# A gated block in eight steps: GpSimd's low parts behind VectorE's mixes, one low part moved to VectorE, another order in the first step

## The reference

```
emb  = layernorm(x) + ctx
q, k, v = emb@wq + bq, emb@wk + bk, emb@wv + bv
ek   = exp(k - max_t k);  ew = exp(w - max w),  w = pos_bias inside a band of 64
y    = sigmoid(q) * (ew @ (ek*v)) / (ew @ ek)
a    = layernorm(y@wo + bo + emb) * gamma + beta
x1   = x + tanh(g_xattn) * (layernorm(relu(a@w1 + b1)@w2 + b2 + a) * gamma + beta)
xn   = layernorm(x1);  xp = xn shifted down by one row
xk   = mu_k*xn + (1-mu_k)*xp;  xr = mu_r*xn + (1-mu_r)*xp
out  = x1 + tanh(g_ffn) * sigmoid(xr@W_r) * (square(relu(xk@W_k)) @ W_v)
```

## Time and profile before

| | |
|---|---|
| median of 3 runs | 509.66 us (509.17 to 512.01) |
| profiled execution, its own time | 508.8 us |
| its span, first to last instruction | 507.1 us |
| busy: TensorE products, weight loads | 450.7 us (89%), 402.5 us (79%) |
| busy: VectorE, GpSimd, ScalarE | 433.1 (85%), 303.7 (60%), 234.3 us (46%) |
| mean granted clock of TensorE | 0.963 of 2.4 GHz |
| DMA | 48.27 MB, 95 GB/s |

### The profile page before, as it was taken

One profiled execution on the slowest core, in us unless ns is written; L12 is line 12 of the kernel. 1 busy time (PEld: TensorE's weight loads), 2 busy tenths in 40 slices (PEclk: granted clock), 3 DMA queues, 4 the chain that ended last, 5 costly groups with the idle time before them and its releaser, 6 DMA issues. The chain is left out here.

```text
span 507.1 us, 8069 instructions
## 1 busy us (share of the span) xinstructions
PE 450.7 (89%) x2884; PEld 402.5 (79%) x2884; DVE 433.1 (85%) x768; ACT 234.3 (46%) x366; POOL 303.7 (60%) x242
## 2 busy tenths in 40 slices
PE   7889997779979897998979998898979996999986
PEld 7778896669869795997869796897959885897975
DVE  4998779699888999699996999789986997279987
ACT  3581653515264343825255343834255242536353
POOL 2573862386765786675775786665773653744431
PEclk9999999699989999899989999899999997999999
DMA  7742210446023820347114650244212330011002
GB/s 259 241 126 83 63 43 2 129 141 197 1 83 98 244 88 0 106 166 197 41 50 128 189 145 0 91 134 161 84 41 53 124 120 7 1 41 43 2 0 84
DMA packets 44216, 48.27 MB, mean 95 GB/s; under 512 B 8592, under 2 KB 40336, under 8 KB 44176
## 3 DMA queue, kind: packets, MB, share of 16 engines
q1 hardware_dynamic: 43088, 46.18, 29.3%
q10 hardware_dynamic: 1088, 1.57, 1.0%
HBM read 31.29 MB, written 16.45 MB: 94 GB/s over the span
## 5 line engine op out<-in xcount | busy, mean ns | idle before, releaser
L1682 PE MATMUL ps<-w_hi,hid_hi 128*128 128x256 f32 x248 | 61.6, 284 | 0.8 <-issue 0.5
L1682 PE MATMUL ps<-a_hi,w_hi 128*128 128x512 f32 x128 | 52.9, 414 | 9.9 <-DVE hid_lo L1070 7.0
L1682 PE MATMUL ps<-w_lo,hid_hi 128*128 128x256 f32 x248 | 61.0, 282 | 0.0
L1496 ACT ACTIVATE hid_hi<-ps,b 128x512 fp32r<-128x512 f32 x60 | 37.9, 686 | 39.7 <-PE ps L1682 39.7
L923 DVE RECIPROCAL y<-y 128x512 f32<-128x512 f32 x16 | 53.6, 3350 | 0.3
L1682 PE MATMUL ps<-a_hi,w_lo 128*128 128x512 f32 x128 | 52.3, 409 | 0.0
L1070 DVE SCALAR_TENSOR_TENSOR hid_lo<-ps,neg_b,hid 128x512 fp32r<-128x512 f32 x60 | 41.2, 736 | 10.8 <-ACT hid L1502 10.8
L1682 PEld LDWEIGHTS ps<-w_hi,hid_hi 128*128 128x128 f32 x248 | 47.1, 190 | 1.7 <-issue 1.2
L1682 PEld LDWEIGHTS ps<-w_lo,hid_hi 128*128 128x128 f32 x248 | 47.0, 189 | 0.4
L237 POOL TENSOR_TENSOR ek_lo<-y,ek_hi 128x1024 fp32r<-128x1024 f32 x13 | 31.2, 2402 | 21.3 <-ACT ek_hi L1472 21.3
L1682 PE MATMUL ps<-a_lo,w_hi 128*128 128x512 f32 x128 | 36.3, 406 | 4.4 <-POOL a_lo L237 4.4
(11 more groups left out here) (265 smaller groups left out, 1405.8 us busy)
## 6 DMA issues: line engine op xcount, KB each, us to landing
x_in<-in_x SPq DMA_DIRECT2D x8, 512.0 KB, 4.3
emb<-in_ctx SPq DMA_DIRECT2D x8, 512.0 KB, 3.8
x_beta<-in_x SPq DMA_DIRECT2D x8, 512.0 KB, 4.7
out<-out_sb SPq DMA_DIRECT2D x7, 512.0 KB, 4.3
key_room<-norm SPq DMA_DIRECT2D x6, 512.0 KB, 2.6
y<-key_room SPq DMA_DIRECT2D x24, 128.0 KB, 2.9
mid_room<-hid SPq DMA_DIRECT2D x6, 512.0 KB, 2.6
hid<-mid_room SPq DMA_DIRECT2D x24, 128.0 KB, 2.9
```

What stands on the lines that cost most here:

```text
L1496: act.activation(tile(hi, b, T), bank(relu_pair(n, q), b), ACT.Relu, bias=b1[:, m:m + 1]).then_inc(hid_hi_done, 1)
L1682: return pe.matmul(o, s, m, start=start, stop=stop, skip_group_check=True)
```

## The change

On GpSimd the three low parts of a step's middle wait for both of VectorE's mixes (`xr_done`) and run in the order xk, xr, y; `ek_low` waits for `x1_done` and comes after `stats("ff")`; `a_square_low` leaves GpSimd for VectorE, between `scale_ff` and `finish_x1`. On TensorE the wait for `ek_done` moves ahead of `hidden(b,3)` and the wait for the hidden low parts ahead of `values`, and in the last step `hidden(b,2)` comes before `ffn_k`. In the first step (`i == FIRST_MID`) VectorE, ScalarE, SyncE and GpSimd take the attention sum, the mid norm and its turn first and the head norm, the keys' turn and sums after them; `hidden(0,3)` gets other banks, and the counts of the stores follow the new order.

```diff
--- before.py
+++ after.py
@@ -290,15 +290,15 @@
 
         def keys_stored(n):
 
-            return 16 * (STORES * (n - FIRST_EK) + 1)
+            return 16 * (STORES * (n - FIRST_EK) + (2 if n == FIRST_EK else 1))
 
         def sums_stored(n):
 
-            return 16 * (STORES * (n - FIRST_EK) + 2)
+            return 16 * (STORES * (n - FIRST_EK) + (3 if n == FIRST_EK else 2))
 
         def mid_stored(n):
 
-            return 16 * (STORES * (n - FIRST_MID) + 3)
+            return 16 * (STORES * (n - FIRST_MID) + (1 if n == FIRST_MID else 3))
 
         def emb_stored(n):
 
@@ -381,7 +381,9 @@
 
             if is_last(n):
                 return (0, 2, 1, 0)[q]
-            return (0, 2, 1, 0)[q] if isinstance(n, int) and n == BATCH - 2 else (0, 2, 0, 0)[q]
+            if n == 0:
+                return (0, 2, 0, 1)[q]
+            return (0, 2, 1, 0)[q] if n == BATCH - 2 else (0, 2, 0, 0)[q]
 
         def value_pair(n):
 
@@ -561,12 +563,16 @@
                 load_unit(sp, u)
 
             def step(i, p):
-                if has(i + 1):
+                if i == FIRST_MID:
+                    load_ctx(i + 2, p)
+                    spread_mid(i)
                     spread_keys(i + 1)
                     spread_sums(i + 1)
-                if has(i + 2):
-                    load_ctx(i + 2, p)
-                if mid_squares(i):
+                elif not is_last(i):
+                    spread_keys(i + 1)
+                    spread_sums(i + 1)
+                    if has(i + 2):
+                        load_ctx(i + 2, p)
                     spread_mid(i)
                     sp.wait_ge(mid_landed, mid_moved(i))
                 if has(i + 2):
@@ -703,13 +709,14 @@
                     emb_plus_bo(d, 1 - p)
                 if has(a):
                     delta_of(pool, a)
-                if has(a) and is_last(i):
+                if has(a):
+                    pool.wait_ge(xr_done, DC * (a + 1))
                     xk_low(pool, a)
                     xr_low(pool, a)
                 y_low(pool, i)
-                if has(a) and not is_last(i):
-                    xk_low(pool, a)
-                    xr_low(pool, a)
+                if i == FIRST_MID:
+                    stats("mid", i)
+                    scale_a(i, p)
                 if has(e):
                     stats("head", e)
                 if has(a) and is_last(i):
@@ -717,18 +724,19 @@
                 x_plus_beta(b)
                 if has(a) and not is_last(i):
                     sq_low(pool, a)
-                stats("mid", i)
+                if i != FIRST_MID:
+                    stats("mid", i)
                 if has(e):
                     pool.wait_ge(norm_done["mid"], TT * (i + 1))
                     make_emb(pool, e, p)
-                scale_a(i, p)
+                if i != FIRST_MID:
+                    scale_a(i, p)
                 if is_last(i):
                     finish_a(i, p)
+                stats("ff", b)
                 if has(d):
+                    pool.wait_ge(x1_done, TT * (b + 1))
                     ek_low(pool, d)
-                stats("ff", b)
-                if mid_squares(i):
-                    a_square_low(pool, i)
                 stats("fin", b)
 
             run_steps(pool, step)
@@ -855,7 +863,7 @@
             def turn_key_squares(n):
 
                 dve.wait_ge(mid_turned, 1)
-                dve.wait_ge(a_scaled_done, 1)
+                dve.wait_ge(a_scaled_done, 2 if n == FIRST_EK else 1)
                 dve.wait_ge(ek_done, DC * (n + 1))
                 for c in range(DC):
                     dve.transpose(ek_blocks.rearrange("p (b x c i) -> p c b x i", b=NB, x=TT, c=DC)[:, c],
@@ -976,7 +984,7 @@
 
                 after(dve, fin_turned, DC * (n - 1))
                 dve.wait_ge(nmr_done["mid"], n + 1)
-                if n > 0 and has(n + 1):
+                if n > FIRST_MID and has(n + 1):
                     dve.wait_ge(room_filled, keys_stored(n + 1))
                 normalise_tiles("mid", res, range(TT - FIRST_DVE, TT))
 
@@ -1160,23 +1168,32 @@
                 if i == 1:
                     unit_low(6)
                     unit_low(7)
-                if has(e):
+                if i == FIRST_MID:
+                    attention_sum(i, p)
+                    hidden_low(b, 2)
+                    normalise_mid(i)
+                    turn_mid_squares(i)
+                    hidden_low(b, 3)
                     head_stats(e)
-                if has(d):
                     turn_key_squares(d)
-                if has(a):
+                    sum_keys(d)
+                else:
+                    if has(e):
+                        head_stats(e)
+                    if has(d):
+                        turn_key_squares(d)
                     square(a)
-                if has(d):
-                    sum_keys(d)
-                hidden_low(b, 2)
-                attention_sum(i, p)
-                if not is_last(i):
-                    normalise_mid(i)
-                hidden_low(b, 3)
-                if is_last(i):
-                    normalise_mid(i)
-                else:
-                    turn_mid_squares(i)
+                    if has(d):
+                        sum_keys(d)
+                    hidden_low(b, 2)
+                    attention_sum(i, p)
+                    if not is_last(i):
+                        normalise_mid(i)
+                    hidden_low(b, 3)
+                    if is_last(i):
+                        normalise_mid(i)
+                    else:
+                        turn_mid_squares(i)
                 if has(a):
                     gate_ffn(a)
                     make_out(a)
@@ -1189,6 +1206,8 @@
                 ff_sum(b, 1 - p)
                 ff_stats(b)
                 scale_ff(b)
+                if mid_squares(i):
+                    a_square_low(dve, i)
                 finish_x1(b)
                 fin_stats(b)
                 if has(d):
@@ -1356,7 +1375,7 @@
                     act.wait_ge(mid_turned, mid_turns(n + 1))
                     act.wait_ge(a_scaled_done, n + 2)
                 act.wait_ge(nmr_done[kind], n + 1)
-                if kind == "mid" and n > 0 and has(n + 1):
+                if kind == "mid" and n > FIRST_MID and has(n + 1):
                     act.wait_ge(room_filled, keys_stored(n + 1))
 
                 for a in range(fin_tiles(n) if kind == "fin" else 0, TT - FIRST_DVE if kind == "mid" else TT):
@@ -1592,12 +1611,18 @@
                 if has(a) and not is_last(i):
                     tanh_r(a)
                     square_high(a)
-                if has(e):
+                if i == FIRST_MID:
+                    hidden_high(b, 3)
+                    normalise("mid", i, res)
                     normalise("head", e, x_in)
-                if has(d):
                     ek_high(d)
-                hidden_high(b, 3)
-                normalise("mid", i, res)
+                else:
+                    if has(e):
+                        normalise("head", e, x_in)
+                    if has(d):
+                        ek_high(d)
+                    hidden_high(b, 3)
+                    normalise("mid", i, res)
                 if has(d):
                     sums_high(d, 0)
                     exp_q(d, 2)
@@ -2047,7 +2072,9 @@
                     pe.wait_ge(sq_done, a + 1)
                 pe.wait_ge(y_hi_done, i + 1)
                 rows_out(2, unit(1, 1), y_hi, y_lo, y_lo_done, i + 1, wo_done)
-                relus_read(NQ * b + 3)
+                pe.wait_ge(ek_done, DC * (d + 1))
+                if has(a):
+                    relus_read(NQ * b + 3)
                 hidden(b, 3)
                 if has(a):
                     ffn_v(a)
@@ -2055,20 +2082,19 @@
                 add_hidden(b, 3)
                 pe.wait_ge(res_done, i + 1)
                 queries(d, 2)
-                pe.wait_ge(ek_done, DC * (d + 1))
                 if has(a):
                     pe.wait_ge(gated_done, a + 1)
+                relus_read(NQ * i)
                 values(d, 1)
-                relus_read(NQ * i)
                 hidden(i, 0, DC * i)
                 pe.wait_ge(exp_q_done, DC * (d + 1))
                 hidden(i, 1)
 
             def last_step_products(i, a, b):
 
-                ffn_k(a)
                 pe.wait_ge(den_read, DC * BATCH)
                 hidden(b, 2)
+                ffn_k(a)
                 ffn_r(a)
                 pe.wait_ge(sq_done, a + 1)
                 pe.wait_ge(tanh_r_done, a + 1)
```

## The result

The changed kernel takes **485.69 us** (median of 4 runs, 484.75 to 486.07) against 509.46 us of the kernel before (4 runs): a ratio of 0.952, interval 0.949 to 0.955. The forecast was 486.0, range 476 to 500. The profiled execution took 485.85 us, its span 484.0.

A forecast was written before the change was run, and what follows sets the result against it. GpSimd's `y_lo` overlapping VectorE's r mixes, delaying TensorE, was taken as the middle steps' bound. 508.8 − 25.5 − 2.7 + 4.3 = 484.9 us profiled, 485.8 as median, stated as 486.0; range 476 to 500.

The forecast's parts named there:

- What bounds the kernel: Middle steps: GpSimd's `y_lo` overlapping VectorE's r mixes costs 4.26 us and causes TensorE's paired waits of 1.24 and 2.28.
- The total: Whole kernel: 484.9 us for the profiled execution, 485.8 for the median, stated as 486.0.
- the 0.9 that the forecast added: Whole kernel: the median of the runs shown lies 0.9 us above the profiled one.
- The middle steps, 5.1 a step: Steps i = 2 to 6: next D at D+52.8 instead of 57.95, gaining 5.1 us a step, 25.5 in all.
- GpSimd's queue of 13.7 us: Middle steps: low parts, head statistics, `x_beta` and `sq_lo` run from D+18.95 to D+32.65, putting the norm at D+34.45.
- The rival of half the gain: Middle steps: GpSimd backlog or a collision with `a_lo` or `make_out` takes 2.5 of 5.1 us; 500 us, chance 0.28.
- `a_lo` on VectorE: Middle steps, before `finish_x1`: the moved low part takes 1.2 us, or 3.6 if held behind a GpSimd instruction.
- The rule that spoke against it: `a_lo` on VectorE has two SBUF inputs, so a working GpSimd could cost it up to a whole GpSimd instruction more.
- thin cover of 0.15 us: Middle steps: VectorE's new wait for ScalarE's `a_hi` ahead of `a_square_low` was put at 0.15 us.
- The last step: Step i = 7: `hidden(b,2)` fills 2.8 of TensorE's 4.00 us wait for `xk_hi`; gain 2.7, bounds 1 and 4.
- The first step: Step i = 1: one TensorE wait of some 9 us, VectorE's values six us late; loss 4.3, bounds 3 and 6.
- The rival that gained from the first step: First step: sums' transfers 6 us sooner shrink both waits and slow clock, gaining some 7; 474.5 us, chance 0.08.

The follow-up runs named there:

- experiment 2: The changed kernel without GpSimd's wait for the mixes and with the old order, `y_lo` first: 507.15 us, ratio 0.995.
- experiment 7: The kernel before with one edit alone, GpSimd's wait for the mixes and the order xk_lo, xr_lo, y_lo: 490.46 us, ratio 0.958.
- experiment 8: The changed kernel with SyncE's `load_ctx` one place ahead of `spread_sums` in the middle steps: 480.38 us, ratio 0.943.
- Experiment 5: The changed kernel; first step only, ScalarE's `exp_q` and `a_high` precede keys and sums, VectorE's queue through fin statistics precedes `sums_low`: 475.67 us, ratio 0.933.
- experiment 9: The changed kernel with `x_plus_beta` behind the mid statistics on GpSimd in steps 2 to 6: 488.48 us, ratio 0.958.

## Why the prediction was right

**What bounds the kernel.** Confirmed by experiments 2 and 7: the overlap of `y_lo` with the r mixes was the root of the waits for `gate_q`, and of the fallen clock behind them. With the waits the clock of the 7 us behind them was 0.76 before and 0.54 in experiment 2; without them it is 1.00 after and in experiment 7.

**The total** is nearer than its terms, and that is luck. In the pair of profiles the errors are −1.0 (the start), +1.6 (first step), +0.6 (middle steps) and −0.3 (last step), 0.9 us together, and the 0.9 that the forecast added for the median over the profiled run wasn't there this time: the profiled run after is 0.2 above its median.

**The middle steps, 5.1 a step.** Each number of the chain can be held against the trace. The r mixes end at D+18.93, forecast and measured (195.68 − 176.75). GpSimd's queue of 13.7 us from there put the norm at D+34.45; it starts at D+34.35. From the norm to the end of `keep_values` 18.2 were forecast; in experiment 8, where nothing collides, the period is 52.43, and 52.43 − 34.35 = 18.1. So the forecast of 52.8 was right for the mechanism to 0.4 us. The mean period after is 264.56 / 5 = 52.91, and this is two errors that cancel: 0.9 us a step of collision that I hadn't placed, and periods of 52.4 with a last one of 50.97 that are shorter than mine.

**The rival of half the gain** was partly at work. It named `make_out`, and `make_out` was hit in three steps of five, though at 0.3 to 1.2 us and not 2.5. Its reason against, that GpSimd is idle at the places I worked out, failed at one: I had left `make_emb` where it was. In the kernel before it starts when ScalarE's norm is done; in the faster step the transfer behind `spread_sums` comes last, and it is pushed into `make_out` or `sums_low`. The prediction counted GpSimd's queue up to the mid norm and, of what comes behind it, looked only at `ek_lo` and the fin statistics.

**`a_lo` on VectorE.** 1.2 was taken between 1.2 and 3.6: it takes 1.21 in step i=3, 1212 ns at the mean of six. The rule that spoke against it found no instruction of GpSimd beside it. Its thin cover of 0.15 us held: VectorE waits 0.6 us for `a_hi` in all.

**The last step**, 2.7 forecast, 3.0 measured. TensorE's timeline after, to be held against the earlier trace rows:

```profile
407.50 0.47 PE L1707 MATMUL ps<-xk_hi,w_hi 128*128 128x512 f32 x1 [1.19 <-ACT xk_hi L1464]
...
411.17 1.19 PE L1707 MATMUL ps<-xk_lo,w_hi 128*128 128x512 f32 x4 [1.58 <-POOL xk_lo L237]
```

4.00 became 1.19, the forecast 4.00 − 2.8, and a new wait of 1.58 for the low part stands behind it ("a little early").

**The first step** is the term that was mis-sized: +4.3 forecast, bounds 3 to 6, and +5.9 measured. The chain itself was right step by step: the key store at 97.63 (98), the sums' last issue at 105.70 (105.2), `a_hi` at 110.73 (110.6), and these rows of VectorE's timeline, to be held against the earlier trace rows:

```profile
109.72 0.42 DVE L917 TENSOR_TENSOR sums_r<-sums_raw,sums_r 4x256 fp32r<-4x256 f32 x1 [11.57 <-ACT sums_r L1441]
...
116.17 1.21 DVE L237 TENSOR_TENSOR a_lo<-hid,a_hi 128x1024 fp32r<-128x1024 f32 x1
...
120.73 1.19 DVE L827 TENSOR_TENSOR res<-ps,bv_rows 128x1024 f32<-128x1024 f32 x1
```

`keep_values` ends at 121.92, forecast 121.9. What was missed is that TensorE, not VectorE, sets D of i=2. TensorE's timeline after, first step, to be held against the earlier trace rows:

```profile
111.41 0.79 PE L1707 MATMUL ps<-a_hi,w_hi 128*128 128x512 f32 x1 [10.67 <-ACT a_hi L1498]
...
117.43 2.07 PE L1707 MATMUL ps<-a_lo,w_hi 128*128 128x512 f32 x4 [2.25 <-DVE a_lo L237]
```

There are two waits and not one. `a_lo` stands on VectorE behind `sums_low`, the ff sum and its statistics, which all waited for the sums: it is ready at 117.38. The waits are 12.9 us together against 6.12 + 2.92 = 9.0 before, 3.9 more. And the products behind the long wait are slow. Windows of the kernel after, columns as in the earlier trace rows:

```profile
111.40:117.40 6.00, 3.78 (x8) 2.48 (x8) 5.89 (x18) 0.47 (x1) 1.27 (x2) 0.50 0.81 247
117.40:124.00 6.60, 6.57 (x16) 5.16 (x17) 6.29 (x17) 3.27 (x5) 4.04 (x5) 0.53 0.31 94
```

and of the kernel before, from the same product on:

```profile
112.00:119.10 7.10, 7.00 (x24) 5.66 (x25) 6.76 (x19) 3.02 (x6) 4.42 (x5) 0.78 0.93 276
```

The 24 products that start with `a_hi` take 124.03 − 111.41 − 2.25 = 10.4 us, at a clock of 0.50 to 0.53 (1.2 GHz nearly throughout), against 119.16 − 112.10 = 7.1 at 0.78: 3.3 more. 3.9 + 3.3 = 7.2; the rest of the step is 1.3 shorter, which makes the 5.9. In that rest lay the slow stretch behind the old wait of 6.12: from 91.95 to 98.95 the granted clock was 0.56 before, and after it is 1.00 from the start of the step to the long wait.

How slow the 24 products are varies from trace to trace. The same windows of experiment 8, whose first step is the same:

```profile
111.40:117.40 6.00, 3.62 (x8) 2.48 (x8) 5.89 (x18) 0.51 (x1) 1.27 (x2) 0.72 0.78 246
117.40:124.00 6.60, 6.53 (x27) 5.40 (x27) 6.29 (x18) 3.23 (x5) 4.05 (x5) 0.74 0.31 94
```

There they take 9.0 us, and the step 59.15: 4.6 more than before, with the end of `keep_values` at 121.96 against 121.92. So some 1.3 of the 5.9 is how long the clock stayed low in this one profile, and the forecast of 4.3 looks nearer in that trace than its working deserves. My 4.3 came from VectorE's lateness alone, less what I thought would be absorbed; it had neither the second wait of TensorE nor the clock behind the long one, which I did count in the middle steps. The rival that gained from the first step fell, for its stated reason: the sums came no sooner. Experiment 5 shows that it didn't need them sooner, but `a_hi` and the rest of VectorE's queue ahead of them: its first step is 48.79 us, 5.8 less than before, with the sums at 110.65.

## What to carry to other kernels

When VectorE's two-input instructions show a wide spread of durations at one shape, look at what GpSimd runs at the same time, and move GpSimd's work before anything else: the order of three calls was worth some 20 us here. Then follow GpSimd's queue through the whole new step, transfers included: the next collision sat 5 us behind the last instruction that I had followed it to. When one engine's order is changed for the sake of another, change it on every queue that the same data pass through; half done, it cost 5 us in the first step, and done it gave 5.

## What the runs showed of the hardware that was not expected

- A `tensor_scalar` with one input in SBUF, 128x256 in float32, is held by GpSimd too: 0.41 us became 2.41 (experiment 9), and 1.93 in the last step of the kernel before.
- A very small instruction is held as long as a large one: `sums_low` reads 4x256 and took 2.51 us instead of 0.42. The size of the victim said nothing of its price here; what was left of GpSimd's instruction did.
- It goes both ways: `make_emb` began 0.18 us behind `make_out`, which kept its 1.28 us, and took 3.36 us instead of 2.40, that is about the rest of `make_out` longer.
- Not held in any of these traces were the statistics, the transposes and the reductions of VectorE: in step i=3 after, `sq_lo` on GpSimd (206.91 to 209.32) lies over the statistics of `res`, which take 1.41 as elsewhere. Over all thirteen kernels a transpose of 128x512 takes 0.66 to 0.72 us.
